# Tiles of 256 tokens stream 384 columns through TensorE in a mixture-of-experts stage

## The reference

```
xn  = layernorm(x)
out = x + attention(xn) + ffn(xn)          # attention: 16 heads of 8, causal

def _expert(h, g, u, d):                   # g, u: 352 x 128, d: 128 x 352
    return einsum('...i,hi->...h', silu(h @ g.T) * (h @ u.T), d)

probs = softmax(xn @ wr.T + rb)            # 7 routed experts
scores, idx = top_k(probs, 2); scores /= scores.sum()
ffn = _expert(xn, shared) + sum over e of w_e * _expert(xn, routed e)
```

## Time and profile before

| | us |
|---|---|
| median of 3 runs | 493.74 |
| lowest and highest of them | 488.05, 497.64 |
| the profiled execution's own time | 489.57 |
| its span, first to last instruction | 487.8 |
| PE busy in the span | 441.3 (90%) |
| DVE busy | 374.9 (77%) |
| ACT busy | 299.6 (61%) |
| POOL busy | 292.6 (60%) |

### The profile page before, as it was taken

One profiled execution on the slowest core, in us unless ns is written; L12 is line 12 of the kernel. 1 busy time (PEld: TensorE's weight loads), 2 busy tenths in 40 slices (PEclk: granted clock), 3 DMA queues, 4 the chain that ended last, 5 costly groups with the idle time before them and its releaser, 6 DMA issues.

```text
span 487.8 us, 12356 instructions
## 1 busy us (share of the span) xinstructions
PE 441.3 (90%) x3983; PEld 326.6 (67%) x3987; DVE 374.9 (77%) x906; ACT 299.6 (61%) x633; POOL 292.6 (60%) x415
## 2 busy tenths in 40 slices
PE   8988799888999999999888999998989899989995
PEld 4765455555666666666565688776868778868884
DVE  6995998898878888888774477574866788756987
ACT  2636577666767676767667676564655765645652
POOL 1445887888887888888888301734537486565200
PEclk9999999989999999999999999999999999999999
DMA  8885799998875555656365216776657677631762
GB/s 238 246 256 195 246 335 313 306 314 277 264 250 146 157 173 163 185 163 182 103 192 221 89 51 218 247 254 239 239 180 270 231 245 255 236 136 36 234 211 67
DMA packets 53215, 102.00 MB, mean 209 GB/s; under 512 B 10245, under 2 KB 28426, under 8 KB 48928
## 3 DMA queue, kind: packets, MB, share of 16 engines
q1 hardware_dynamic: 48672, 92.73, 59.1%
q0 software_dynamic: 4480, 8.47, 5.2%
HBM read 62.49 MB, written 39.46 MB: 209 GB/s over the span
## 4 chain that ended last, share of the span: by engine, by line
PE 59%; DVE 11%; issue 8%; ACT 6%; POOL 5%; DMA 1%; another core or an unknown queue 1%; DVEq 0%; ACTq 0%; SPq 0%; POOLq 0%
PE ps L805 11%; PE ps L803 11%; PE ps L804 10%; PE ps L871 5%; PE ps L932 5%; PE ps L879 4%; ACT sb_work L673 3%; DVE sb_blockmax L1279 3%; POOL xs L584 2%; POOL sb_work L608 2%; PE ps L952 2%; PE ps L1095 2%; PE ps L935 2%; DVE sb_v_all L1388 1%; DVE sb_ring L1395 1%
## 5 line engine op out<-in xcount | busy, mean ns | idle before, releaser
L673 ACT ACTIVATE sb_work<-ps 128x768 f32<-128x768 f32 x128 | 104.4, 816 | 68.6 <-PE ps L867 67.3
L1279 DVE TENSOR_REDUCE sb_blockmax<-ps 128x6 f32<-128x768 f32 x128 | 122.2, 957 | 24.8 <-PE ps L879 18.7
L629 POOL DMA_INDIRECT ys<-sb_v_all,sb_xn_all x76 | 78.7, 1036 | 90.5 <-DVE sb_v_all L1409 68.9
L608 POOL TENSOR_SCALAR_AFFINE_SELECT sb_work<-sb_work 128x512 f32<-128x512 f32 x128 | 82.2, 644 | 30.1 <-ACT sb_work L673 27.6
L804 PE MATMUL ps<-sb_ring,sb_wb 128*128 128x512 f32 (+1 forms) x231 | 83.0, 359 | 0.0
L1388 DVE TENSOR_TENSOR sb_v_all<-ps,sb_v_all 128x512 f32<-128x512 f32 (+1 forms) x93 | 57.5, 618 | 17.7 <-PE ps L805 7.0
L584 POOL DMA_INDIRECT xs<-sb_xn_all,sb_posu x64 | 62.6, 978 | 10.7 <-issue 10.7
L871 PE MATMUL ps<-sb_ring 32*128 32x256 f32 x256 | 49.4, 375 | 15.8 <-ACT sb_work L673 9.8
L753 ACT ACTIVATE sb_v_all<-ps 128x512 f32<-128x512 f32 (+1 forms) x93 | 49.6, 533 | 13.2 <-PE ps L805 6.7
L803 PE MATMUL ps<-sb_ring,sb_wb 128*128 128x512 f32 (+1 forms) x138 | 51.5, 373 | 5.6 <-issue 3.7
L871 PEld LDWEIGHTS ps<-sb_ring 32*128 32x128 f32 x256 | 25.5, 182 | 39.6 <-issue 37.6
(11 more groups left out here) (165 smaller groups left out, 1073.3 us busy)
## 6 DMA issues: line engine op xcount, KB each, us to landing
sb_wb<-wd SPq DMA_DIRECT2D x25, 1152.0 KB
sb_ring<-qk SPq DMA_DIRECT2D x64, 256.0 KB
wd<-sb_wb SPq DMA_DIRECT2D x8, 1152.0 KB, 5.8
xs<-sb_o_all SPq DMA_DIRECT2D x19, 260.0 KB, 3.6
qk<-sb_ring SPq DMA_DIRECT2D x32, 128.0 KB
sb_work<-ys SPq DMA_DIRECT2D x16, 256.0 KB, 3.1
sb_xn_all<-xs SPq DMA_DIRECT2D x15, 260.0 KB
sb_o_all<-w SPq DMA_DIRECT2D x8, 384.0 KB, 3.6
```

The lines of the kernel that those rows point to most:

```text
L608: pool.affine_select(out=o, in_=o, compare_op=ALU.is_ge, fill=0.0, base=0, pattern=[[0, 4], [1, 128]], channel_multiplier=-1)\
L629: pool.indirect_dma_start(out=ys_d, out_offset=bass.IndirectOffsetOnAxis(ap=row, axis=0), in_=yst[i % NYS][:, EMB * j:EMB * j + EMB], in_o ...
L673: act.activation(part.rearrange("p (k h q) -> p h k q", h=2, q=128), ps[:, 4:6, 0:HEAD].rearrange("p h (k q) -> p h k q", q=128), ACT.Exp, ...
L1279: dve.tensor_reduce(blockmax[:, a:b + 1, 0:3], ps[:, a:b + 1, 0:HEAD].rearrange("p h (k c) -> p h k c", c=128), AX.X, ALU.max).then_inc(s[ ...
```

## The change

A new function `streamed(i)` gives the columns that PE streams in a tile: 384 in a small tile, 512 as before in a full one. Gate and up (`half`) and `down` use it for the streamed operand and for the PSUM output. In a small tile the columns 256 to 383 of `xth`, `xtl`, `hh` and `hl` hold what an earlier tile left there; the products of these columns go into columns 256 to 383 of G, U and Y, which nothing reads. ACT, DVE, POOL and SP keep `columns(i)`, their instructions are the same as before, and so is every wait.

```diff
@@ -80,6 +80,12 @@
+def streamed(i):
+
+
+    return max(columns(i), 384)
 
@@ -1015,14 +1021,14 @@
             def tokens(i):
                 r, c = routed(i), shared(i)
                 if r is not None:
-                    return xth[r % 2][:, 0:columns(i)], xtl[r % 2][:, 0:columns(i)]
+                    return xth[r % 2][:, 0:streamed(i)], xtl[r % 2][:, 0:streamed(i)]
...
-                mm3(out[:, 0:columns(i)], wh[:, cols], wl[:, cols], *tokens(i), True, True).then_inc(s[ev], 1)
+                mm3(out[:, 0:streamed(i)], wh[:, cols], wl[:, cols], *tokens(i), True, True).then_inc(s[ev], 1)
@@ -1056,7 +1062,7 @@
             def down(u):
                 i, m = u // MT, u % MT
-                z = columns(i)
+                z = streamed(i)
```

## The result

The changed kernel took 496.15 us (median of 4 runs, 495.02 to 497.25), the kernel before in the same comparison 491.97 (488.05 to 497.64). The ratio is 1.0139, with a 95% interval of 1.0093 to 1.0185: 1.4% slower, within 2%. The profiled executions took 496.12 and 489.57 us, 6.55 apart; that is the distance to explain, where I had forecast 3.4.

The account below looks back on a forecast made before the run. PE, busy 90% of the span, was taken to bound the kernel. Of 12.5 us added, 3.4 remain outside waits: 489.57 + 3.4 = 493.0 us, or 497 us on the median's footing; range 491 to 504.

Parts of the forecast that it names:

- What bounds the stage: Tile stage: PE's own pace plus a list of waits, together 13.6 us.
- The price of a column: Small tiles' 216 matmuls: 128 more columns cost 0.058 us each, 0.175 us at 384 columns, 12.5 us on PE.
- The granted clock has nothing to win: Tile stage: granted clock is 1.00 in all fourteen windows, so the added activity has no clock to win.
- The waits inside small tiles: Inside small tiles PE waits on other engines' backlog from the full tile; waits of 0.10 to 1.67 us swallow columns.
- The waits between small tiles: Between small tiles, waits are tied to POOL's scatter burst and shrink as PE arrives later, hiding up to 0.87 us each.
- The first rival: Waits between small tiles follow PE's own deliveries and keep their length; only waits inside hide columns: +6.0 us, chance 0.25.
- the footing: Whole time: the median of the runs shown, 493.74, 4.2 us above the profiled execution, turning 493.0 into 497 us.
- Nothing is hidden: Small tiles: later product ends push waits out as far as PE, so all columns cost: +12.5 us, 2.5%, chance 0.09.

Follow-up runs that it names:

- the second group's chip: Kernel before and changed kernel rerun on one other chip, 476.89 and 484.47 us, ratio 1.0184; both also run there without the 76 scatters, stages 188.12 and 200.33 us.
- the six traces: Traces with late hand-overs: both kernels of the first comparison; in the third group the kernel before (489.95 us), small weight loads, and both kernels with loads in thirds (497.35, 510.05).

## Why the prediction was right, and where it was not

*What bounds the stage:* right. PE's pace plus a list of waits describes both traces of the comparison, and other chips need one more item, PE at its lower clock; the floor is 188.1 us, and 203.92 - 188.1 = 15.8 us of waits stand against the 13.6 that I read from the windows of the routed tiles.

*The price of a column:* right. Forecast 12.5 us for 216 matmuls; 12.21 without scatters, and a spacing of 0.177 us where 0.175 was estimated.

*The granted clock has nothing to win:* right here, 1.00 in all windows of both kernels. On the second group's chip it had an estimated 1.5 us to win, at 319.43 us, and the changed kernel lost none there.

*The waits inside small tiles:* right in effect. Six of 1.27, 0.44, 0.79, 0.95, 1.40 and 0.10 us are gone in the changed kernel, and the eighth tile's fell from 1.67 to 1.01. The cause that I gave, ACT's and DVE's backlog from the full tile, was incomplete: without scatters, on the second group's chip, they aren't there either. And the largest that I set down to it, tile 19's 1.40, has another: at 400.47 us DVE's low part took 2.02 us beside a POOL operation of 1.32 at 400.61, and PE waited 1.19 us for it.

*The waits between small tiles:* wrong, and this is the step that was mis-sized. "The burst is POOL's own length, so PE arrives later at the wait behind it and waits less" gave 4 x 0.87 = 3.5 us behind tiles 4, 7, 10 and 13. The four waits sum to 7.4 us where there were 6.95: nothing was taken, and 3.4 + 3.5 = 6.9 would have been the sum, against 6.55 measured on the profiled executions. The ground I had for it was a coincidence of times, 0.55 us three times between a burst's end and a small tile's start. Both followed DVE's work in that stretch: POOL's last pair of scatters waited for DVE's result of the small tile before, PE for DVE's parts of the full tiles and of the next tokens. In the changed kernel the pair's wait grew from 1.02 to 3.84 us, and the 0.55 us were gone.

*The first rival* (these waits keep their length, +6.0) had the place and the size right, and was given 0.25. That the number 497 lies 0.85 us from the measured median is luck: the sum was 3.1 us short (3.4 against 6.55), and the footing was 1.8 us high, since the median of the kernel before moved from 493.74 to 491.97 with one more run. By the ratio the change is 1.4% and not 0.7%.

*Nothing is hidden* was wrong with scatters and right without them (12.21 us against 12.5), which is the best evidence that waits did hide the rest.

What stays open: why PE's hand-overs come late beside scatters on some chips. Weight loads are not the main part of it (14.1 us above the floor without them). That scatters are needed is argued from their place in the six traces; the kernels without scatters ran only on a chip without late hand-overs.

## What to carry to other kernels

Work added to the engine that bounds a stage costs its full price less the waits that it can reach, and a wait is reached only if what ends it doesn't move along; measure the floor by taking the disturbing transfers out, then count waits above it, and look at the granted clock behind the long ones. A fixed distance between two events names a common cause, not which of them sets the other: before a wait is called tied to a queue's clock, look whether that queue itself waited for the same engine inside the stretch. And a tuned kernel's waits may belong to the chip that it ran on: here 204 us and 195 us of stage for one program.

## What was not expected of the hardware

- The same program took 491.97, 476.59, 476.89 and 489.95 us in four comparisons, 3% apart by chip. Most of it stands in the tile stage: 15.8 us above the floor in one trace, 7.3 in another.
- On the slower chips semaphore hand-overs from PE to ACT and DVE came up to 3.2 us late while indirect scatters ran (a silu 4.21 us behind its matmul's start against 0.43 in the changed kernel), with PE's own rows running on at their usual spacing of 0.23 us. On the faster ones not one was late by more than 0.10 us.
- Behind a wait of 1.89 us PE ran at granted clock 0.50 from 319.43 to 322.61 us, an estimated 1.5 us on top of the wait.
- Cutting a 1152 KB load into three of 384 KB, two of them issued earlier, cost 1.5% where it was to win 1%.
